# Step sizes: a second PSUM place for the logarithm and every other u on GpSimd; last layer: its gate weights loaded in the stencil layer

## What is computed

```python
dlt = jnp.einsum('bkrl,kdr->bkdl', dlt, dt_proj_w) + dt_proj_b[None, :, :, None]
dlt = jax.nn.softplus(dlt)
dA = dlt[..., None] * A_log[None, :, :, None, :]
dbx = dlt[..., None] * jnp.swapaxes(b, 2, 3)[:, :, None] * xs[..., None]
```

```python
def _mlp(v, w1, b1, w2, b2):
    return jax.nn.relu(v @ w1.T + b1) @ w2.T + b2
def _gate(g, half):
    go, gi = (g[:, :half], g[:, half:])
    return jax.nn.sigmoid(go[:, :, None] * gi[:, None, :])
Y0 = _gate(_mlp(x_0.mean((2, 3)), gsp_w1, gsp_b1, gsp_w2, gsp_b2), C0)
x_0 = _group_conv(x_0, conv0_w[None] * Y0[..., None, None], conv0_b, 1)
```

## Time and profile before

| | us |
|---|---|
| median of 3 runs (2972.81 to 2978.46) | 2978.03 |
| the profiled execution's own time | 2974.61 |
| its span in the profile | 2972.7 |

### The profile page before, as it was taken

One profiled execution on the slowest core, in us unless ns is written; L12 is line 12 of the kernel. 1 busy time (PEld: TensorE's weight loads), 2 busy tenths in 40 slices (PEclk: granted clock), 3 DMA queues, 4 the chain that ended last, 5 costly groups with the idle time before them and its releaser, 6 DMA issues. The chain is left out here.

```text
span 2972.7 us, 24549 instructions
## 1 busy us (share of the span) xinstructions
PE 2162.6 (73%) x7460; PEld 1057.5 (36%) x7460; DVE 2552.8 (86%) x2138; ACT 1575.5 (53%) x2301; POOL 1939.5 (65%) x645
## 2 busy tenths in 40 slices
PE   6853566676766666776666677678985999798579
PEld 3421223333332333333323333334432555354444
DVE  5678899999999999999999999986887777699620
ACT  1565677777777777777776777753230000362220
POOL 0165899999999999999999999984000000297000
PEclk9977799999999999999999999998897999899689
DMA  1276444444454444445444454535005443100360
GB/s 48 88 221 235 119 111 115 111 125 121 107 129 110 120 117 114 119 108 129 109 118 123 112 125 100 125 84 180 0 1 153 115 116 96 38 8 16 78 88 24
DMA packets 140258, 308.71 MB, mean 104 GB/s; under 512 B 47643, under 2 KB 63264, under 8 KB 135136
## 3 DMA queue, kind: packets, MB, share of 16 engines
q1 hardware_dynamic: 139040, 303.01, 40.3%
q10 hardware_dynamic: 1088, 4.13, 0.6%
HBM read 220.30 MB, written 46.87 MB: 90 GB/s over the span
## 5 line engine op out<-in xcount | busy, mean ns | idle before, releaser
L842 POOL TENSOR_TENSOR l0c_r<-l0c_r,l0c_v 128x1536 f32<-128x1536 f32 x288 | 990.6, 3447 | 51.1 <-DVE l0c_r L804 49.3
L879 ACT ACTIVATE ps<-l0c_dlt,l0c_na 128x512 f32<-128x512 f32 (+1 forms) x1152 | 626.1, 575 | 474.6 <-DVE l0c_h L830 460.1
L830 DVE TENSOR_TENSOR_SCAN l0c_h<-ps,l0c_h,l0c_r 128x768 f32<-128x768 f32 x384 | 693.3, 1806 | 1.2 <-issue 0.6
L851 POOL TENSOR_TENSOR l0c_hcp<-l0c_cb,l0c_h 128x1536 f32<-128x1536 f32 x198 | 682.9, 3449 | 1.4 <-issue 1.4
L762 PE MATMUL ps<-l0c_hcp,net_ident 128*128 128x512 f32 (+1 forms) x1584 | 586.6, 493 | 17.6 <-ACT l_Z L872 7.1
L889 ACT ACTIVATE l0c_r<-l0c_S,l0c_floor,l0c_na 128x768 f32<-128x768 f32 x576 | 580.1, 1014 | 18.0 <-issue 18.0
L729 PE MATMUL ps<-l0c_Bp,l0c_sel 96*128 96x512 bf16 (+1 forms) x1152 | 289.3, 333 | 379.5 <-DVE l0c_r L804 180.3
L804 DVE SCALAR_TENSOR_TENSOR l0c_r<-l0c_r,ps 128x768 f32<-128x768 f32 x576 | 533.1, 926 | 6.6 <-PE ps L729 3.9
L762 PEld LDWEIGHTS ps<-l0c_hcp,net_ident 128*128 128x128 f32 x1584 | 272.1, 192 | 268.7 <-issue 195.7
L830 DVE TENSOR_TENSOR_SCAN l0c_h<-ps,l0c_r 128x768 f32<-128x768 f32 x192 | 335.0, 1745 | 0.0
L1541 PE MATMUL ps<-l_prod,l_wa 128*96 128x384 f32 (+1 forms) x888 | 291.8, 492 | 25.8 <-DVE l_prod L1458 25.8
(11 more groups left out here) (273 smaller groups left out, 2286.2 us busy)
## 6 DMA issues: line engine op xcount, KB each, us to landing
l0c_cb<-cf SPq DMA_DIRECT2D x396, 384.0 KB, 5.5
l_other<-l_p SPq DMA_DIRECT2D x22, 864.0 KB, 5.9
dlt<-l0s_dl SPq DMA_DIRECT2D x36, 384.0 KB, 2.3
v<-l0s_vv SPq DMA_DIRECT2D x36, 384.0 KB, 2.9
l0c_dlt<-dlt SPq DMA_DIRECT2D x36, 384.0 KB, 3.4
l0c_v<-v SPq DMA_DIRECT2D x36, 384.0 KB, 4.5
l_other<-l_p SPq DMA_DIRECT2D x22, 288.0 KB, 6.7
l0c_Bp<-bc SPq DMA_DIRECT2D x36, 144.0 KB, 3.7
```

The lines of the kernel that those rows point to most:

```text
L830: dve.tensor_tensor_scan(h[:, n, :], da[j % 2], r[:, j % NR, :], init, ALU.mult, ALU.add).then_inc(s_scan, 1)
L842: pool.tensor_tensor(two, two, v[:, (j // N) % 2, :].unsqueeze(1).to_broadcast([128, 2, SEG]), ALU.mult).then_inc(s_w, 2)
L851: pool.tensor_tensor(hcp[:, p % NHP:p % NHP + 2, :], cb[:, p % NCB:p % NCB + 2, :], h[:, e % N:e % N + 2, :], ALU.mult).then_inc(s_hp, 2)
L879: act.activation(da[e % 2][:, part], dlt[:, i, part], ACT.Exp, scale=na[:, i, n:n + 1]).then_inc(done, 1)
```

## The change

In l0_steps: x has two places in all units (`base`), so X(i) waits for S(i-2). The third place becomes a second place for the logarithm from unit 8 on (`log_slot`, `log`), and Ln(i) waits for D(i-2) in place of D(i-1). u of odd units moves from DVE to POOL (`negative_u`), the same tensor_scalar; on POOL it stands in front of the v of the unit before: u(i+1), v(i), v(i+1), and in front of `turned` of its round.

In layer 3: the seven weights and four matrices are loaded by SP in l2_diffuse, behind its row loads. The bias row of the second layer becomes a 33rd row of w2, with a 1 in the hidden layer, so two matmuls fall away. The six spread DMAs move into l3_forward's SP list, behind its three loads, and the two edge memsets onto its POOL list.

```diff
         def base(i):
-            return (0, 2, 6)[slot(i)] * BANK
+            return (0, 2)[i % 2] * BANK
+        def log_slot(i):
+            return 0 if i < SECOND else (i - SECOND + 1) % 2
+        def log(i):
+            o = (4, 6)[log_slot(i)] * BANK
+            return ps[:, o:o + SEG]
...
-                    pe.wait_ge(s_s, before(i) + 1)
+                    pe.wait_ge(s_s, i - 1)
...
-                    if i >= 2:
-                        act.wait_ge(s_dl, i - 1)
-                    act.activation(ps[:, LN:LN + SEG], u[:, (i - 1) % NW, :], ACT.Ln, scale=-1.0).then_inc(s_ln, 1)
+                    if before(i - 1) is not None:
+                        act.wait_ge(s_dl, before(i - 1) + 1)
+                    elif log_slot(i - 1):
+                        act.wait_ge(s_bce, 2 * NC)
+                    act.activation(log(i - 1), u[:, (i - 1) % NW, :], ACT.Ln, scale=-1.0).then_inc(s_ln, 1)
...
-                    if by_vector(i):
-                        if i >= NW:
-                            dve.wait_ge(s_q, i - NW + 1)
-                        dve.tensor_scalar(u[:, i % NW, :], e[:, i % NE, :], -1.0, -1.0, ALU.mult, ALU.add
-                                          ).then_inc(s_uv, 1)
...
+            def negative_u(i):
+                pool.wait_ge(s_e, i + 1)
+                if i >= NW:
+                    pool.wait_ge(s_q, i - NW + 1)
+                pool.tensor_scalar(u[:, i % NW, :], e[:, i % NE, :], -1.0, -1.0, ALU.mult, ALU.add).then_inc(s_up, 1)
+
             turned(0)
             for i in range(U):
+                if i == 0:
+                    negative_u(1)
+                elif by_pool(i + 1) and i + 1 < U:
+                    negative_u(i + 1)
...
+            for dst, src in ahead:
+                sp.dma_start(dst, src).then_inc(s_ahead, 16)
             for tl, p0, ch0, n, b, hf in pieces:
                 sp.wait_ge(s_all, tl + 1)
...
-                pe.matmul(ps[0:1, (1 + b) * BANK:(1 + b) * BANK + GO], hid[:, b:b + 1], w2[:, :],
-                          start=True, stop=False)
-                mm = pe.matmul(ps[0:1, (1 + b) * BANK:(1 + b) * BANK + GO], one[:, 0:1], b2[:, :],
-                               start=False, stop=True)
+                mm = pe.matmul(ps[0:1, (1 + b) * BANK:(1 + b) * BANK + GO], hid[:, b:b + 1], w2[:, :],
+                               start=True, stop=True)
...
             sp.dma_start(bwc[:, :], a["bwc"]).then_inc(s_in, 16)
+            for i in range(3):
+                lo, hi = max(0, 1 - i), L - max(0, i - 1)
+                for b in range(B):
+                    sp.dma_start(G0[C3 * i:C3 * i + C3, b, :, :].rearrange("c h w -> c (h w)")[:, W + lo:W + hi],
+                                 XG[0:C3, b, lo + i - 1:hi + i - 1]).then_inc(s_spread, 16)
```

More of the change, by code:

```diff
@@ L485, in _ @@
                         act.wait_ge(s_s, i - NE + 1)
-                        if by_vector(i - NE):
-                            act.wait_ge(s_uv, (i - NE) // 2 + 1)
+                        if by_pool(i - NE):
+                            act.wait_ge(s_up, (i - NE) // 2 + 1)
                     act.activation(e[:, i % NE, :], ps[:, base(i):base(i) + SEG], ACT.Abs).then_inc(s_ab, 1)
-                if i and not by_vector(i - 1):
+                if i and not by_pool(i - 1):
                     act.wait_ge(s_e, i)
@@ L1552, with l2_diffuse @@
 DVE_TAPS, POOL_TAPS = 36, 19
-def l2_diffuse(nc, ps, X, pad, ident, kern):
+def l2_diffuse(nc, ps, X, pad, ident, kern, ahead):
     NT = KS * KS
@@ L1714, in l3_gates @@
         whole_t = sb("whole", [128, 2, H], I32)
-        (s_in, s_dve, s_gap, s_hid, s_hs, s_row, s_rs, s_gate, s_gs, s_als, s_fr, s_cs, s_x
-         ) = map(sem, "in dve gap hid hs row rs gate gs als fr cs x".split())
-        s_tr, s_zero, s_pad, s_spread = map(sem, "tr zero pad spread".split())
-        NIN = 7
-        NTR = 4
+        (s_dve, s_gap, s_one, s_hid, s_hs, s_row, s_rs, s_gate, s_gs, s_als, s_fr, s_cs, s_x
+         ) = map(sem, "dve gap one hid hs row rs gate gs als fr cs x".split())
+        s_tr, s_pad = map(sem, "tr pad".split())
         block = ctx.enter_context(nc.Block())
@@ L1811, in _ @@
             step = Steps(dve, s_dve)
-            step(dve.memset(one[:, :], 1.0))
+            dve.memset(one[:, :], 1.0)
+            dve.memset(hid[HC:HC + 1, :], 1.0).then_inc(s_one, 1)
             step(dve.tensor_tensor(gap[:, :], st["mv"][:, :, 0], st["rstd"][:, :], ALU.mult))
@@ L1837, in _, with l3_forward @@
             dve.wait_ge(s_cs, 1)
-def l3_forward(nc, a, ps, wg, ws, cs, d, tr):
+def l3_forward(nc, a, ps, wg, ws, cs, d, tr, XG, G0):
     with ExitStack() as ctx:
@@ L1857, in l3_forward @@
             sem, "in mm ea ed ph m1 m2 v vst mst".split())
+        s_spread, s_zero = sem("spread"), sem("zero")
         block = ctx.enter_context(nc.Block())
@@ L1899, in _ @@
             sp.wait_ge(s_mst, 16)
+        @block.gpsimd
+        def _(pool):
+            pool.wait_ge(s_spread, 96)
+            pool.memset(G0[0:C3, :, 1:1 + H, 0:1], 0.0).then_inc(s_zero, 1)
+            pool.wait_ge(s_zero, 1)
+            pool.memset(G0[2 * C3:3 * C3, :, 1:1 + H, W - 1:W], 0.0).then_inc(s_zero, 1)
+            pool.wait_ge(s_zero, 2)
         @block.tensor
@@ L2261, in l3 @@
                 group_norm(nc, "gn3", X, ps, gavg, st, [by_image(XG[:, b, :]) for b in range(B)])
-                l3_gates(nc, a, ps, st, wg, ws, w0g, cs, d, XG, G0, tr)
-            l3_forward(nc, a, ps, wg, ws, cs, d, tr)
+                l3_gates(nc, ps, st, wg, ws, w0g, cs, d, XG, G0, tr, w)
+                l3_forward(nc, a, ps, wg, ws, cs, d, tr, XG, G0)
         l3_inverse(nc, a, ps, X, G0, w0g, d, out)
@@ L2320, in program @@
                 group_norm(nc, "gn2", X, ps, gavg, st, [interior(pad[:, b, :, :], RAD) for b in range(B)], edges)
-                l2_diffuse(nc, ps, X, pad, ident, kern)
+                l2_diffuse(nc, ps, X, pad, ident, kern,
+                           [(whole(w3[n]), a[n]) for n in ("w1", "b1", "wt", "w0", "lv", "ef2", "fh2", "ef", "fw")]
+                           + [(w3["w2"][0:HC, :], a["w2"]), (w3["w2"][HC:HC + 1, :], a["b2"])])
         if 3 in layers:
-            l3(nc, a, ps, X, gavg, st, out)
+            l3(nc, a, ps, X, gavg, st, out, w3)
         else:
```

78 lines of the change are left out of this document (26 added, 52 removed).

## The result

| | before | after |
|---|---|---|
| median of the runs measured together | 2975.42 us (4 runs, 2972.61 to 2978.46) | 2952.60 us (4 runs, 2947.46 to 2955.26) |
| the profiled execution's own time | 2974.61 us | 2952.53 us |
| its span | 2972.7 us | 2950.6 us |

What follows compares the result with a forecast made beforehand. DVE was taken to bound steady l0_steps pairs, stores its middle, and DMA l3_gates. Gains of 6.0 + 11.5 = 17.5 us off 2978.0 gave 2960.5 us, range 2950 to 2971.

Steps and rivals of the forecast that it cites:

- Whatever either stage gives up comes off the span in full: l0_steps and l3_gates each end in a barrier, so time saved in either shortens the whole run by as much.
- The loop through POOL, 4.84 + c, closes a pair: Steady l0_steps pairs: D, v, u on POOL, Ln, Q, D limit a pair, 6.34 us against 7.12 before.
- c = 1.5 us: Time of one u on POOL in l0_steps, estimated from other POOL rows, with ends 0.7 and 3.6 us.
- The sum's own formula: Gain of l0_steps: 1.8 + 8 x (7.12 - 4.84 - c) - 2.1 = 18.0 - 8c, 6.0 us.
- rival (a): l0_steps: GpSimd is quick, c near 1.0 or less; stage gains 9 to 10, total 21, 2957 us; chance 0.17.
- The rule against the edit: For u on POOL in l0_steps: the skill's page sends elementwise work to VectorE, as GpSimd is slower.
- The floor of 5.9 us a pair: l0_steps: DVE and the run Ln to S, Q keep pairs from going much below 5.9; gain at most 10 us.
- Two places for x: l0_steps: X(i) waits for S(i-2), a loop of 5.1 or 6.4 us by clock; price nothing to 0.1 us a pair.
- S(16) 1.0 us and S(20) 1.8 us sooner: Store-bound middle of l0_steps: DVE freed of u reaches S(16) 1.0 us and S(20) 1.8 us earlier, ends 0 and 4.
- `turned` in the loop: l0_steps round 26: the copy on POOL lengthens one pair to about 9 us, a net loss of 2.1 us.
- u behind last_part: l0_steps: u(15) stands behind last_part and v(13) on POOL, covered by S(16)'s DMA wait; uncovered it costs 0.8 us.
- Layer 3, 11.5 us: l3_gates: the stage ends with `xh` instead of the edge memsets, 11.5 us sooner, ends 10.5 and 14.5.

Runs made afterwards that it cites:

- The halves: Only the l0_steps edits, or only the layer 3 edits, applied to the kernel before: 2964.82 us (ratio 0.9968) and 2961.90 us (ratio 0.9957).
- the doubled u: The changed kernel with each u of odd units made twice on POOL, first into a spare tile: 2956.19 us.
- u before v: The changed kernel with POOL's order made v(i), u(i+3), v(i+1) for even i: 2946.27 us, ratio 0.9903 to the kernel before.

## Why the prediction was right, and which term was off

The direction, the order of the terms and the range (2950 to 2971) held; the gain was 5.3 us larger than forecast. By its own steps:

- **"Whatever either stage gives up comes off the span in full"**: right as far as the noise tells. The halves add up (9.5 and 12.4 against 22.8). That the scan between them takes 1934.8 and 1934.9 us is luck in part, since it varies from 1933.4 to 1938.4 over the profiles.
- **The loop through POOL, 4.84 + c, closes a pair**: right, shown by the doubled u (6.37 against 6.46) and by u before v, which ends ACT's waits for POOL in steady pairs.
- **c = 1.5 us**: this is the step that failed. It is 0.83. The value was taken "next to the copy, which like u has one input". But a third of the `turned` copy is no copy of 768 columns: that instruction also exchanges rows and columns (whether this makes it slow was not tested). The lower bound, half of the memset, 0.69, was the nearer row. The sum's own formula with the measured c gives 18.0 - 8 x 0.83 = 11.4 us, and the stage gave 12.0: the formula holds, its one unknown was mis-sized. That it comes so close is luck in part: up to S(20) 3.0 us were gained where the formula has 1.8, from there on 9.0 where it has 9.5. A c near 1.0 or less was rival (a), with 0.17.
- **The rule against the edit**: the GPSIMD Engine Reference of the Trainium skill (section 3.1) gives 1.8 cycles per element as the best case of the loop, an estimated 1.15 us; measured is 0.83, less than that, though 1.15 is nearer than 1.5. The same section also gives 1.03 cycles per element for a loop bound by its ports, an estimated 0.66 us; the measured time lies between the two. The rule of its section 4.1 that sends elementwise work to VectorE would have forbidden the best part of the change, 9.9 us; the same table adds that a single-input operation runs at roughly line rate on GpSimd, and this trace agrees in the main: 0.83 us stands beside 0.80 to 0.92 for ACT's instructions of the same width, and above the 0.55 that DVE takes at best. The prediction weighed the rule and overlooked that half of it.
- **The floor of 5.9 us a pair, from "DVE and the run Ln, E, S, Q, D, S, Q"**: wrong. u before v runs at 5.29 to 5.45. In DVE's timeline of that kernel S starts at 234.69, Q at 235.56, D at 236.54 and the next S at 237.42: each starts 0.87 to 0.98 us behind the one before, though each is recorded as 0.95, and a pair needs 5.45 us, near the 5.4 that the prediction itself had for DVE's work.
- **Two places for x, "nothing to 0.1 us a pair"**: too low. The loop was named, with 6.4 us at the lower clock, but it was priced as if it cost nothing beside POOL's loop of 6.34. Beside the real loop of 5.67 it shows: 6.16 us in the pair in which Abs waits 0.77 us for x, and 6.37 against 5.30 in the two executions of u before v.
- **S(16) 1.0 us and S(20) 1.8 us sooner**: low. Counted from the stage's start, and by one profile of each, S(16) comes 1.2 us sooner (212.55 - 210.55, less the 0.8 by which the stage starts earlier) and S(20) 3.0 (226.52 - 222.69, less 0.8).
- **`turned` in the loop, a pair of about 9 us**: right, 8.44; the rule 4.1 + 3.64 + c + the rest gives 4.84 + 0.83 + 2.9 = 8.57.
- **u behind last_part**: seen, for u(9), at a cost of a 2.68 us wait of ACT and 2.12 of DVE; like u(15) it is followed by the waits for stores, and no run tells what it costs.
- **Layer 3, 11.5 us**: 13.5, within its bounds of 10.5 to 14.5. The stage ended 13.9 us behind the start of `g`, where `xh` alone was given 15.1: alone on the queue it lands in 5.6 us (median of four), against 6.8 behind the eleven loads, so "the last of four was the slow one" was too careful. The gate chain ended 10.2 us behind `g` ("at the latest" 12.5).
- **Spread and loads hidden at no cost**: right. The first store of V stands at the same 36.4 us, the layers between at +0.2.
- **Costs nobody asked about**: layer 1 +2.7 and the end +1.1. The end varies between 175.7 and 178.6 us over all fourteen profiles, that of before among them, with no tie to an edit. Layer 1 is told below.

Of the signs that were named, the pair of 6.0 to 6.6 us came only in part: of the seven pairs without `turned` four took 5.52 to 5.87 us and three 6.12 to 6.16, the first of these behind a store, the second behind x, the third behind POOL. A pair below 5.6, which was to prove the argument wrong, came three times. It does not prove that: 4.84 + 0.83 lies at 5.67. The sign hung on the same c and should have been written as 4.84 + c.

## What to carry to other kernels

When two engines share a chain of instructions, find the fuller one and take an instruction off it first; the further buffer gave less (each alone 9.9 and 4.2 us here, and the buffer 2.1 on top of the move). When work moves to another engine's in-order queue, write down the loop that its position closes and place it where that loop doesn't contain it: the same instruction one place earlier gave 2.7 us more. And write a sign of being wrong in terms of what you had to guess, so that a guess that is off doesn't look like a wrong mechanism. At a stage's end, see what ends last, and move out what the next stage needs only later (9.7 us) before speeding up what it waits for (3.8 us).

## What the runs showed of the hardware

- A one-input tensor_scalar of 768 fp32 columns takes 0.83 us on POOL, beside DVE instructions that read PSUM, and on DVE 0.55 alone, and 0.81 to 3.65 us beside POOL (the median of all 18 is 1.16 us before, 1.53 with the second place of the logarithm alone). The Trainium skill, SBUF — State Buffer, section "SBUF: two separate sides", tells of a port pair that one of the two engines holds for its whole instruction; the 3.65 us, ending 0.41 us behind POOL's instruction, agree. Moved to POOL, that instruction pays nothing, while the DVE instructions left, with an input in PSUM, stay at 0.95.
- Layer 1 takes 314.3 us in eight profiles, 317.1 in four (the changed kernel and its repeat among them), 316.0 in one, and 314.4 before, with the same instructions. In the view by stretch the difference is TensorE's clock as PE takes up work: first after, then u before v in the first of its two executions.

```profile
2258.70:2263.70 5.00, 2.21 (x6) 0.88 (x4) 4.72 (x2) 0.00 (x0) 0.00 (x0) 0.84 0.99 236
2263.70:2268.70 5.00, 4.56 (x7) 2.09 (x8) 2.95 (x2) 0.00 (x0) 0.00 (x0) 0.50 1.02 243
2268.70:2273.70 5.00, 5.00 (x15) 2.52 (x14) 4.56 (x2) 0.00 (x0) 0.00 (x0) 0.89 1.03 251
```

```profile
2258.50:2263.50 5.00, 1.80 (x6) 0.68 (x4) 4.78 (x2) 0.00 (x0) 0.00 (x0) 0.99 0.99 236
2263.50:2268.50 5.00, 4.61 (x15) 2.38 (x16) 2.89 (x2) 0.00 (x0) 0.00 (x0) 1.00 1.02 243
2268.50:2273.50 5.00, 5.00 (x17) 2.59 (x16) 4.70 (x2) 0.00 (x0) 0.00 (x0) 1.00 1.05 251
```

  In the stretch from 2263.7 the changed kernel's granted clock is 0.50 (1.2 GHz) and it does 7 matmuls, where the other is at 1.00 (2.4 GHz) and does 15, with DVE and DMA alike. In the stretch before, PE had been partly idle in both (busy for 2.21 and 1.80 of 5 us). With that one drop more the layer ends 2.7 us later. All five longer ones are kernels with edits in both stages, and neither half alone shows it (314.3 us each); but six others with edits in both don't show it either, and u before v took 314.3 us in one execution and 316.0 in the next. So whether the change makes it likelier is not shown, and what makes it come was not found.
- Cutting a store did not bring its first part in sooner: SP goes on 4.45 us behind the issue of 1152 KB, and 4.3 us behind that of its first half with the second half queued behind.
